# A two-layer decoder on one core: an order planned with tile shapes, top rows turned at full width, roots at both ends on ScalarE and VectorE

## The chip, the cores and the metric

The kernel runs on one core of a Trainium2 chip. Its engines are TensorE (matmuls into eight PSUM banks), VectorE, ScalarE, GpSimd and SyncE, which here issues nearly all DMAs. The metric is the device time of one execution in microseconds; lower is better.

## The reference

The input is x of 4 x 256 x 256 (batch, position, feature) and a context of 4 x 256 x 64. Six blocks follow one another, each added to its input and then normalised over the features (`layernorm(x + block(x))`):

1. latent attention with 32 heads: a projection to 192 query and 64 + 64 key values, a root-mean-square norm of both latents, rotated parts, causal softmax, output weights;
2. a mixture x = (1 - gamma) x + gamma A, where A is the symmetrised sigmoid of a similarity from the context, kept only where it is among the 76 largest of its row;
3. eight experts (one shared, seven routed, two chosen for each token), each up, silu gate, down;
4. causal attention with 16 heads of 16 values, with biases and rotation;
5. a bilinear block: softmax of a normalised similarity, scaled by rows gamma and beta;
6. a gated feed-forward with 1024 hidden values.

The last normalised x is the output. All is float32.

## The kernel before

All 1024 tokens stay in SBUF as 8 tiles of 128 rows (two for each batch). Weights come in by DMA, are split into a high and a low part (names ending in `_hi` and `_lo`), and most products are done as three matmuls hi*hi, hi*lo, lo*hi.

The work is written as steps such as `("s", b, g, half)`: scores of two heads of group g in batch b. `make_plan` (L396) declares for each step the engines it visits with an estimated time on each (`"PE 1.31, DVE 1.22, ACT:exp 1.8"`), the steps that it needs, and the buffers (banks, `probs`, `probsT`, ...) it holds. `Plan.arrange` (L301) is a list scheduler: it takes the engine whose next step can start soonest, and among the steps of this engine that can start within `NEAR[engine]` it takes the one with the highest level. The level is the longest chain of work behind the step, plus what the table `URGENT` (L176) adds for its name or its name and indices. The result is one order of steps for each engine, `ORDER`. `write_program` then emits for each engine its steps in this order; engines meet only by semaphores, so each engine works strictly in its order and stalls where a step isn't ready.

Steps that matter here, by the parts of the array their matmuls use:
- full width (128 rows, 128 columns): projections `q`, scores `s`, transposes `pT`, output `out`, experts `e_*`, `qkv`, `qkT`, feed-forward `f_*`;
- 128 rows, 64 columns: `w_v` (weights of values and output multiplied), `pv` (probabilities times the latent), `bi_kv`;
- 64 rows, 128 columns: `adj_sim`, `s1` and `st1` (scores of the second attention, once by rows for the maxima, once transposed for the exponentials), `ctx_tok`, `bi_sim`;
- 128 rows, 32 columns: `route_lin`, `pv1`;
- 64 rows, 64 columns: `adj_qk`, `ctx_T`.

In the planner before, TensorE knows nothing of these shapes. `NEAR["PE"]` is 0.

Top rows: `s1` writes the maxima of the rows of four heads into `top_tok` (128 x 2 x 4). `top_split` negates and splits them into `top_rows`, `top_T` transposes them (two transposes of 128 x 8, one for each row tile), ScalarE copies the result to `topT` (8 x 256), and four DMAs put it into rows of `qT1`, where `st1` uses it.

Roots: `down` computes the latents and their sums of squares (two halves h = 0, 1). `down_root` takes the reciprocal root on GpSimd: `power` with the exponent -0.5, then one Newton step (`newton_step`, L2384, four instructions). `down_scale` multiplies on GpSimd, ScalarE and VectorE; `down_T` transposes for TensorE. Each normalisation of x does `bn_stats`, `bn_aggr` and a small addition on VectorE (`statistics`, L1901), then `root` (L2355) on GpSimd. For the last batch the two tiles are done singly (`"first tile"`), and VectorE scales all output tiles (`out_norm`), each followed by a DMA to the output.

## Time and profile before

| | |
|---|---|
| time, median of 3 runs | 703.93 us (702.81 to 706.13) |
| span of the profiled execution | 700.4 us, 14717 instructions |
| the profiled execution's own time | not listed beside its span |
| TensorE busy | 680.6 us (97%), 4886 matmuls |
| VectorE, ScalarE, GpSimd busy | 531.1, 494.1, 394.8 us |
| DMA | 41.06 MB, mean 59 GB/s |

Read from a profile of one execution. Busy is the time in which an engine had an instruction in work; matmuls are pipelined and their ends are modelled, so the start times of matmuls are the better clock: the distance between two starts is what the first one cost. `PE` is TensorE, `PEld` its weight loads, `DVE` VectorE, `ACT` ScalarE, `POOL` GpSimd, `SP` SyncE. L1184, L1198, L2338, L2341 and the like are lines of helpers, so a line gathers operations of many steps; the tile names tell them apart.

### The profile page before, as it was taken

Reading aid. Unit: us, or ns where it says so; the run is one execution under the profiler, and the core shown is the slowest. Engines: PE = TensorE matmul, PEld = TensorE weight load, DVE = VectorE, ACT = ScalarE, POOL = GpSimd, SP = SyncE. Lnnn points to the kernel's source line nnn. Section 1 sums busy time; section 2 is a strip of 40 time slices with the busy share of each in tenths; the row PEclk is TensorE's granted clock in tenths of the full one; section 3 lists DMA queues with packets and bytes.
Section 4 is the critical chain, followed back from the end, with each engine's and each line's share of the span. In section 5 each row is a group of like instructions: output and inputs, shape, how many; then the busy total and the mean of one; then the engine's idle time right before and its main releaser. Section 6 shows DMA issues by size and latency. Waiting matters only on the chain.

```text
span 700.4 us, 14717 instructions
## 1 busy us (share of the span) xinstructions
PE 680.6 (97%) x4886; PEld 574.7 (82%) x4886; DVE 531.1 (76%) x1677; ACT 494.1 (71%) x1276; POOL 394.8 (56%) x657
## 2 busy tenths in 40 slices
PE   8899999999999999999998999999989999999995
PEld 6578998888888888888886888898977787678885
DVE  2678989888697869878889776565689777866537
ACT  3789774888659784788879786646766686857631
POOL 4659732885267741698867655544791322435625
PEclk9999999999999999999999999999999999999999
DMA  8671001240341401122012002111120000101201
GB/s 293 167 229 42 17 1 40 53 122 2 109 133 32 122 1 54 46 54 61 2 49 89 1 28 63 47 46 46 46 91 3 5 2 4 48 1 46 91 1 60
DMA packets 34418, 41.06 MB, mean 59 GB/s; under 512 B 6620, under 2 KB 27238, under 8 KB 34344
## 3 DMA queue, kind: packets, MB, share of 16 engines
q1 hardware_dynamic: 33800, 39.80, 19.4%
q8 instruction: 39, 0.64, 0.4%
q10 hardware_dynamic: 544, 0.33, 0.2%
q14 instruction: 35, 0.29, 0.1%
HBM read 30.02 MB, written 1.05 MB: 44 GB/s over the span
## 4 chain that ended last, share of the span: by engine, by line
PE 77%; POOL 9%; DVE 8%; issue 3%; DMA 1%; SPq 1%; ACT 0%; POOLq 0%; DVEq 0%
PE bank L1184 68%; PE bank L1198 8%; POOL stat L2341 3%; POOL qT L2341 1%; PE bank L1455 1%; POOL probs L2338 1%; DMA qT<-xT_plain 1%; DVE top_tok L2238 1%; POOL probs L2341 1%; POOL w_split_lo L2341 1%; DVE g_pair_lo L1896 1%; SPq L2622 1%; DVE y L1899 1%; POOL stat L2338 1%; DVE bn L1911 1%
## 5 line engine op out<-in xcount | busy, mean ns | idle before, releaser
L2338 POOL TENSOR_SCALAR probs<-probs,soft 128x256 f32<-128x256 f32 (+1 forms) x256 | 104.5, 429 | 48.4 <-DVE soft L2031 46.7
L1686 ACT ACTIVATE probs<-probs,soft 128x256 f32<-128x256 f32 (+1 forms) x256 | 113.0, 447 | 13.5 <-DVE soft L2023 12.9
L1184 PE MATMUL bank<-xT_hi,w_split_hi 128*128 128x512 f32 x256 | 103.7, 405 | 3.5 <-POOL w_split_lo L2341 3.2
L2341 POOL TENSOR_TENSOR w_split_lo<-w_raw,w_split_hi 128x512 fp32r<-128x512 f32 (+2 forms) x57 | 72.3, 1275 | 55.1 <-ACT w_split_hi L1592 54.9
L1184 PE MATMUL bank<-xT_lo,w_split_hi 128*128 128x512 f32 x256 | 101.0, 394 | 0.0
L1184 PE MATMUL bank<-keyT,qT 128*128 128x256 f32 (+1 forms) x512 | 93.4, 330 | 0.5 <-POOL qT L2341 0.3
L2023 DVE CUSTOM_DVE_ANT_0 probs<-bank,mask 128x256 f32<-128x256 f32 (+1 forms) x256 | 78.9, 353 | 19.8 <-PE bank L1184 19.1
L1184 PEld LDWEIGHTS bank<-keyT,qT 128*128 128x128 f32 x512 | 81.8, 190 | 12.3 <-issue 2.5
L2341 POOL TENSOR_TENSOR qT<-qT,xT_plain 64x512 f32<-64x512 f32 x44 | 57.0, 1295 | 57.6 <-DMA qT<-xT_plain 55.5
L1184 PE MATMUL bank<-xT_hi,w_split_lo 128*128 128x512 f32 x192 | 75.9, 395 | 0.0
L1592 ACT ACTIVATE qT<-bank 64x512 f32<-64x512 f32 (+1 forms) x80 | 47.4, 592 | 33.1 <-PE bank L1184 30.6
L1592 ACT ACTIVATE probsT<-bank 128x384 f32<-128x384 f32 x128 | 53.9, 490 | 18.6 <-PE bank L1198 18.4
L2341 POOL TENSOR_TENSOR probs<-probs 128x512 f32<-128x512 f32 x32 | 44.3, 1396 | 31.6 <-ACT probs L1769 31.0
L1184 PEld LDWEIGHTS bank<-xT_hi,w_split_hi 128*128 128x128 f32 x256 | 48.5, 190 | 15.5 <-POOL w_split_lo L2341 3.9
L1184 PEld LDWEIGHTS bank<-xT_lo,w_split_hi 128*128 128x128 f32 x256 | 48.6, 190 | 9.0
L2341 POOL TENSOR_TENSOR stat<-stat,power 128x2 f32<-128x2 f32 (+3 forms) x29 | 24.5, 843 | 49.2 <-DVE stat L1892 49.0
L1184 PE MATMUL bank<-probsT,key_tok 128*64 128x256 f32 (+1 forms) x512 | 50.2, 335 | 0.0
L1184 PE MATMUL bank<-w_split_hi,g_pair_hi 128*128 128x256 f32 x176 | 49.9, 284 | 0.3 <-DVE g_pair_lo L1896 0.3
L1198 PE MATMUL bank<-identity,probs 128*128 128x128 f32 x384 | 50.1, 273 | 0.1
L1184 PE MATMUL bank<-w_split_hi,g_pair_lo 128*128 128x256 f32 x176 | 49.4, 281 | 0.0
L1184 PE MATMUL bank<-w_split_lo,g_pair_hi 128*128 128x256 f32 x176 | 49.4, 280 | 0.0
L1686 ACT ACTIVATION_READ_ACCUMULATOR probs<-probs,soft 128x1 f32 x256 | 49.0, 191 | 0.0
(240 smaller groups left out, 1822.0 us busy)
## 6 DMA issues: line engine op xcount, KB each, us to landing
qT<-xT_plain SPq DMA_DIRECT2D x88, 64.0 KB, 2.0
w_raw<-in_w_nopeT SPq DMA_DIRECT2D x8, 512.0 KB, 3.6
w_raw_heads<-in_w_o SPq DMA_DIRECT2D x8, 512.0 KB, 5.1
qT<-rope_buf SPq DMA_DIRECT2D x40, 64.0 KB, 2.0
w_raw<-in_w_gateT SPq DMA_DIRECT2D x8, 256.0 KB, 2.8
w_raw<-in_w_upT SPq DMA_DIRECT2D x8, 256.0 KB, 3.3
w_raw<-in_w_downT SPq DMA_DIRECT2D x8, 256.0 KB, 3.8
w_raw<-in_L_ffn_Wup SPq DMA_DIRECT2D x7, 256.0 KB, 2.8
```

Of the source, the lines that this page charges most:

```text
L1184: return t.matmul(out, lhsT, rhs, start=start, stop=stop, skip_group_check=shared)
L1198: return t.transpose(out, in_, ident[0:rows, 0:rows])
L1455: ins = t.transpose(out[:, t_ * S + i * P:t_ * S + (i + 1) * P].bitcast(F32R), rows_of_head(rows)[:, i, first:first + P], ident1)
L1592: return s.activation(out, in_, ACT.Copy, **kw)
L1686: ins = s.activation(p[:, at], p[:, at], ACT.Exp, bias=st[:, 0, r:r + 1], scale=-1.0, accum_out=st[:, 1, r:r + 1])
L1896: return v.tensor_tensor(out, in0, in1, op)
L1899: return v.scalar_tensor_tensor(out=out, in0=in0, scalar=s, in1=in1, op0=op0, op1=op1)
L1911: own(v.bn_stats(bn[place][:, i, 0:6], tile))
L2023: v.tensor_tensor_reduce(out=p[:, at], in0=bank_of(("s", b, g, h))[:, at], in1=mask, scale=-SCALE0, scalar=3.0e38, op0=ALU.add, op1=ALU.mi ...
L2238: v.reduce_max(top_tok[top1_turns.place[b, g]][:, :, 2 * p + j], two(bank_of(("s1", b, h))), AX).then_inc(top1.sem, 1)
L2338: return g_.tensor_scalar(out, in0, s1, s2, op0, op1)
L2341: return g_.tensor_tensor(out, in0, in1, op)
```

## The change

- `Plan` gets `MODE = 0.13` (us for a TensorE step whose tile shape differs from the step before) and `KEEP = 835` (added to the level of a TensorE step that keeps the shape); `NEAR["PE"]` goes from 0 to 0.15. The small-tile steps are declared with their shape (`PE:cols64`, `PE:rows64`, `PE:cols32`, `PE:quarter`) and with other times. Every entry of `URGENT` is replaced.
- `probsT` has 8 buffers of 128 x 384 in place of 6 of 128 x 512; a group takes four at once, and `pT` of the second half comes after that of the first.
- Top rows: `top_rows` is 128 x 128, zeroed once; its first 16 columns hold high and low parts of both row tiles; one full transpose replaces two.
- `down_root` is split: VectorE forms a quarter of the mean square plus epsilon (`down_var`), ScalarE takes its square root, VectorE makes the reciprocal root from both in four instructions (`root_of_quarter`). The last batch's normalisation does the same, one tile at a time, and its scaling stays on VectorE. The other batches' roots stay on GpSimd, and their output tiles are scaled by ScalarE.
- `last_table`: a square root of one column on ScalarE behind the last `f_up`.
- Some semaphores that signalled one event each are merged.

```diff
-    HOP, TABLE = 0.2, 1.3
-
-    NEAR = {"PE": 0.0, "ACT": 0.3, "DVE": 0.3, "POOL": 0.5, "SP": 0.3, "DMA": 0.1, "WAY": 0.0}
+    HOP, TABLE, MODE = 0.2, 1.3, 0.13
+    KEEP = 835
+
+    NEAR = {"PE": 0.15, "ACT": 0.3, "DVE": 0.3, "POOL": 0.5, "SP": 0.3, "DMA": 0.1, "WAY": 0.0}
...
                     t = max(ready, free[engine], since)
-                    if kind and kind != table:
+                    if engine == "PE":
+                        t += self.MODE * (kind != tile)
+                    elif kind and kind != table:
                         t += self.TABLE
...
+            def stays(step):
+                engine, _, kind = self.parts[step][running[step][0]]
+                return engine == "PE" and kind == tile
+
             t, step, engine, taken = max((c for c in could if c[2] == soonest[2] and c[0] <= near),
-                                         key=lambda c: (level[c[1]], -c[0]))
+                                         key=lambda c: (level[c[1]] + self.KEEP * stays(c[1]), -c[0]))
...
-        stage(("down_root", h), "DVE 0.2, POOL 2.2", ("down", h), ("zero",))
+        stage(("down_var", h), "DVE 0.2, ACT 0.25", ("down", h))
+        stage(("down_root", h), "DVE 0.75", ("down_var", h))
...
-        stage(("w_v", g), "PE 1, ACT 0.6, DVE 0.6", ("load", g), *before,
+        stage(("w_v", g), "PE:cols64 0.8, ACT 0.6, DVE 0.6", ("load", g), *before,
...
-                      + [Hold("probsT", (b, g, h), By(("pv", b, g), "PE")) for h in heads], items=2)
-            stage(("pv", b, g), "PE 1.5, ACT 0.57, DVE 0.6", ("pT", b, g, 0), ("pT", b, g, 1),
+                      + [Hold("probsT", (b, g, h), By(("pv", b, g), "PE")) for h in range(GH) if half == 0], items=2)
+            stage(("pv", b, g), "PE:cols64 1.22, ACT 0.57, DVE 0.6", ("pT", b, g, 0), ("pT", b, g, 1),
...
-                stage(("s1", b, g, p), "PE 0.5, DVE 1.2", ("qkT", b, g), ("consts",),
+                stage(("s1", b, g, p), "PE:rows64 0.46, DVE 1.2", ("qkT", b, g), ("consts",),
...
-            stage(("pv1", b, g), "PE 1.02, ACT 0.45", *[("st1", b, g, p) for p in range(GH // 2)], ("v1", b), *every_expert,
+            stage(("pv1", b, g), "PE:cols32 0.88, ACT 0.45", *[("st1", b, g, p) for p in range(GH // 2)], ("v1", b), *every_expert,
...
+    stage(("last_table",), "ACT:sqrt 0.2", By(("f_up", NHALF - 1, HT - 1), "ACT"))
...
-                for i in range(TB):
-                    ins = transpose(out[0:2 * GH, i * P:(i + 1) * P],
-                                    plain(top_rows[top1_turns.place[b, g]][:, i, :, :]).rearrange("p c h -> p (c h)"))
-                ins.then_inc(topT_ready.sem, 1)
+                transpose(out[:, 0:P], plain(top_rows[top1_turns.place[b, g]][:, :])).then_inc(topT_ready.sem, 1)
...
+            elif name == "down_var":
+                h, = k
+                place = in_stat.place["down", h]
+                w.wait_ge(*low_seeded[h])
+                s.activation(stat[place][:, 2, :], stat[place][:, 0, :], ACT.Sqrt).then_inc(sqrt_taken.sem, 1)
...
+        def root_of_quarter(quarter, half, r):
+
+            own(v.reciprocal(r, half))
+            w.wait_ge(*own.now)
+            own(tt(r, r, quarter, ALU.mult))
+            w.wait_ge(*own.now)
+            own(tt(r, r, half, ALU.add))
+            w.wait_ge(*own.now)
+            return v.reciprocal(r, r)
...
                 for i, t in enumerate(batch_tiles(b)):
-                    w.wait_ge(*(newton["first tile"] if (b, i) == (B - 1, 0) else newton["out_stats", b]))
-                    ts(x[:, t, :], y[:, t, :], bn[place][:, i, 6:7], stat[place][:, 1, i:i + 1], ALU.subtract,
-                       ALU.mult).then_inc(out_normed.sem, 1)
+                    quarter, r, half = (stat[place][:, j, i:i + 1] for j in range(3))
+                    w.wait_ge(*sqrt_taken["last", i])
+                    own(root_of_quarter(quarter, half, r))
+                    w.wait_ge(*own.now)
+                    ts(x[:, t, :], y[:, t, :], bn[place][:, i, 6:7], r, ALU.subtract, ALU.mult).then_inc(last_normed.sem, 1)
```

## Rows read from the trace of the kernel before

**Rows 1.** Busy us and share of each engine; the last chain by engine.

```profile
PE 680.6 (97%) x4886; PEld 574.7 (82%) x4886; DVE 531.1 (76%) x1677; ACT 494.1 (71%) x1276; POOL 394.8 (56%) x657
...
PE 77%; POOL 9%; DVE 8%; issue 3%; DMA 1%; SPq 1%; ACT 0%; POOLq 0%; DVEq 0%
```

**Rows 2.** Windows: stretch, length, busy PE, PEld, DVE, ACT, POOL; clock, DMA, GB/s.

```profile
300.00:350.00 50.00, 50.00 (x390) 43.81 (x388) 41.98 (x171) 42.74 (x144) 43.25 (x82) 1.00 0.14 37
350.00:400.00 50.00, 46.99 (x323) 39.23 (x323) 42.34 (x118) 41.81 (x73) 33.69 (x67) 1.00 0.16 49
...
500.00:550.00 50.00, 46.86 (x445) 38.43 (x443) 43.95 (x93) 31.77 (x69) 29.42 (x34) 1.00 0.16 50
...
650.00:700.40 50.40, 42.49 (x259) 37.62 (x257) 27.01 (x58) 19.22 (x35) 22.50 (x42) 0.97 0.16 53
```

**Rows 3.** TensorE's waits: total us, times, longest.

```profile
PE bank L1184 <- POOL w_split_lo L2341: 3.2, 2, 1.8
...
PE bank L1184 <- ACT topT L1592: 0.5, 1, 0.5
```

**Rows 4.** TensorE in order of time: start, us, tile shape (rows*columns), operands, count.

```profile
17.31 1.08 PE L1184 MATMUL bank<-w_raw_heads 128*64 128x256 f32 x8
...
58.73 0.38 PE L1198 MATMUL bank<-identity,probs 128*128 128x128 f32 x2
59.04 0.66 PE L1184 MATMUL bank<-probsT,key_tok 128*64 128x256 f32 x4
...
61.74 0.38 PE L1184 MATMUL bank<-keyT,qT 128*128 128x128 f32 x2
61.96 0.82 PE L1198 MATMUL bank<-identity,probs 128*128 128x128 f32 x6
...
635.80 1.13 PE L1184 MATMUL bank<-kvT,outT 64*128 64x256 f32 x4
636.86 0.38 PE L1184 MATMUL bank<-w_split_hi,g_pair_hi 128*128 128x256 f32 x1
```

**Rows 5.** The same, in the second attention.

```profile
519.35 0.50 PE L1184 MATMUL bank<-kT,qT 64*128 64x256 f32 x4
...
539.25 0.38 PE L1198 MATMUL bank<-identity,top_rows 128*8 128x128 f32 x2
539.47 0.38 PE L1198 MATMUL bank<-identity,ctx 128*128 128x128 f32 x2
```

**Rows 6.** Single instructions by group: busy us, mean ns (first row: min/median/max ns).

```profile
L1592 ACT ACTIVATE top_rows<-top_tok x16: 191/210/212, 520.6 to 602.9; 128x8 fp32r<-128x8 f32 x16
...
L2253 DVE RECIPROCAL ctx_inv<-bank 128x8 f32<-128x8 f32 x16 | 3.2, 203 | 2.6 <-PE bank L1198 2.2
...
L1892 DVE TENSOR_SCALAR stat<-sums 128x8 f32<-128x8 f32 x2 | 0.3, 165 | 0.1
...
L1592 ACT ACT_TABLE_LOAD x1 | 1.3, 1283 | 1.8 <-issue 1.8
...
L2338 POOL TENSOR_SCALAR probs<-probs,soft 128x256 f32<-128x256 f32 (+1 forms) x256 | 104.5, 429 | 48.4 <-DVE soft L2031 46.7
```

**Rows 7.** The front in order of time; then GpSimd's small steps; then a window.

```profile
19.34 1.85 POOL L2341 TENSOR_TENSOR stat<-stat,power 128x8 f32<-128x8 f32 x1
...
21.20 1.39 DVE L1899 SCALAR_TENSOR_TENSOR xT_lo<-bank,q_ln,xT_hi 128x512 fp32r<-128x512 f32 x2
...
24.66 0.50 PE L1184 MATMUL bank<-xT_hi,w_split_hi 128*128 128x512 f32 x1 [1.82 <-POOL w_split_lo L2341]
...
L2341 POOL TENSOR_TENSOR stat<-stat 128x8 f32<-128x8 f32 x6 | 1.2, 202 | 0.5
...
25.10:28.40 3.30, 3.30 (x10) 2.52 (x9) 1.50 (x3) 0.91 (x2) 2.44 (x5) 0.50 0.29 34
```

**Rows 8.** The tail on VectorE in order of time.

```profile
695.28 0.15 DVE L1892 TENSOR_SCALAR stat<-bn 128x1 f32<-128x1 f32 x1
...
697.75 0.41 DVE L1893 TENSOR_SCALAR x<-y,bn,stat 128x256 f32<-128x256 f32 x1 [1.18 <-POOL stat L2341]
```

More of the change, by code:

```diff
@@ L301, in arrange @@
     def arrange(self):
-        level, ends, starts, table = self.levels(), {}, {}, ""
+        level, ends, starts, table, tile = self.levels(), {}, {}, "", ""
         free = defaultdict(float)
@@ L874, in write_program @@
     bi_exp = signal("bi_exp", keys("sim_max"))
+    out_normed = signal("out_normed", keys("out_norm", range(TB)))
     f_silu = signal("f_silu", keys("f_up"))
@@ L1856, in scalar_program @@
                 norm_rows(("sim_mix", b), batch_tiles(b))
+            elif name == "last_table":
+                w.wait_ge(*landed("identity"))
+                s.activation(last_root[:, 0:1], ident[:, 0:1], ACT.Sqrt)
+            elif name == "out_stats":
+                place = in_stat.place[step]
+                for i in range(TB):
+                    w.wait_ge(*seeded["first tile" if i == 0 else step])
+                    s.activation(stat[place][:, 2, i:i + 1], stat[place][:, 0, i:i + 1], ACT.Sqrt).then_inc(sqrt_taken.sem, 1)
+            elif name == "out_norm":
+                b, = k
+                place = in_stat.place["out_stats", b]
+                w.wait_ge(*newton["out_stats", b])
+                for i, t in enumerate(batch_tiles(b)):
+                    s.activation(x[:, t, :], y[:, t, :], ACT.Identity, bias=stat[place][:, 3, i:i + 1],
+                                 scale=stat[place][:, 1, i:i + 1]).then_inc(out_normed.sem, 1)
             elif name == "bi_kv":
@@ L2422, in pool_program @@
                 g_.memset(router_rows[:, :, :], 0.0).then_inc(zeroed.sem, 1)
-            elif name == "down_root":
-                h, = k
-                ve, r, s_ = (stat[in_stat.place["down", h]][:, j, :] for j in range(3))
-                w.wait_ge(*zeroed["zero"])
-                w.wait_ge(*low_seeded[h])
-                own(tt(r, ve, power[:, :], ALU.pow))
-                newton_step(r, s_, ve).then_inc(low_rsqrt.sem, 1)
             elif name == "down_rope":
@@ L2495, in pool_program @@
                     own(g_.memset(t[:, :, :], 1.0))
+                for t in top_rows:
+                    own(g_.memset(plain(t[:, :]), 0.0))
                 for t in (q_rows, k_rows):
```

276 lines of the change are left out of this document (141 added, 135 removed), and 43 rows, old and new, of the table URGENT.

## The prediction

> **What bounds the kernel now.** I read the engine totals first. TensorE is busy 680.6 of 700.4 us, VectorE 531.1, ScalarE 494.1, GpSimd 394.8 [rows 1]; by engine the chain that ended last is 77% TensorE [rows 1]. So it is a matmul-bound kernel, and an edit is worth what it takes out of TensorE's own stream, out of its waits, or out of the two ends. The windows say where the waits are [rows 2]: 300 to 350 us has none (50.00 of 50 us), 350 to 400 lacks 3.0, 500 to 550 lacks 3.1, and the last 50.4 us hold 7.9 us without a matmul, nearly all of it the tail. The list of waits puts a name to the largest: TensorE waits 3.2 us in two pieces for GpSimd's w_split_lo, 1.8 the longer, and only 0.5 us in all for the copy of the top rows [rows 3]. Full busy time isn't full speed, however, so I went to single matmuls.
>
> **A change of tile shape costs about 90 ns.** Two 128x128 transposes that begin at 61.74 (scores, same shape) are followed by the next group at 61.96: 0.22 us for two, 0.11 each. The two at 58.73 are followed by a 128*64 group at 59.04: 0.31 us, so 0.09 more. On leaving it is no less: the four 64*128 matmuls of 256 columns at 635.80 are followed at 636.86, 1.06 us for four of 0.22 us (twice a 128-column one), 0.18 more, of which I take half for the way out [rows 4]. Going through TensorE's records in order of start I count 183 changes of shape; the first is into the 128*64 group at 17.31 and the last at 636.86 us [rows 4]. Of them 89 lie before 400 us, most around the 128*64 stretches (38 stretches for 40 steps pv and w_v), and 94 between 510 and 637 us, where scores of the second attention (64*128, 33 stretches for 64 steps s1 and st1) alternate with pv1 (128*32, 13 stretches for 16 steps) and full-width work. 183 x 0.09 = 16.5 us of the span is spent on changes, nothing of which shows as idle.
> The Trainium skill (TensorEngine Tiling (Array Packing), Tiling Modes, Key Properties) says that changing the tiling mode drains TensorE; the trace agrees, with the 0.09 us above. By its list of modes a matmul of 8 columns would count as another mode than full width, and here the trace differs for transposes: see the top rows below.
>
> **The change, part by part.**
> *The order.* The planner gets a price of 0.13 us for a changed tile shape, a bonus of 835 on the level of a step that keeps the shape, a window of 0.15 us (before: 0) in which the more urgent TensorE step may be taken, lower prices for small-tile steps, and wholly new urgencies. The number of matmuls stays. What can be merged? Context products come one per (batch, group) and each needs its own two transposes; with room for two groups of transposed probabilities at once (8 places taken four at a time, before 6 taken two at a time) a few more pv and w_v may stand together: I take 4 stretches fewer of 38, 8 changes. In the second attention the 33 stretches often hold one step, four score products and their four masks, as at 519.35 [rows 5], while several steps are ready together whenever a (batch, group) has its rows; there I take 33 to 23 and 13 to 10, 26 changes. Sum 34 x 0.09 = 3.1 us, all on the path, as TensorE has no idle time there that would hide it. Bounds: 0 changes fewer (0 us) and, at the other end, half of all (92 x 0.09 = 8.3 us). Waits between steps are re-dealt by the new order; they can't fall by much more than the 6.1 us of the two stretches with most of them [rows 2], and I take 0, because nothing in the trace says whether the new order is better or worse in this.
> *Top rows at full width.* Now two transposes of 128x8 for each of 16 groups; after: one of 128x128. They cost 0.11 us each: two from 539.25 to 539.47, and the full-width transposes behind them begin without a gap, so they are no change of shape today [rows 5]. The gain is 16 x 0.11 = 1.8 us. The ScalarE copy of the negated maxima (210 ns [rows 6]) and VectorE's keep their size; the copy out has 128 columns for 256; four row DMAs of unchanged bytes stay, from four partitions each for two; three more GpSimd memsets lie in rows1, ahead of the second attention, in which GpSimd works 29.4 of 50 us [rows 2]. Bounds: 0 (if st1 waited for the DMA anyway) to 1.8; I take 1.8, since TensorE's waits of that kind are 0.5 us in all [rows 3].
> By the mode list of the Trainium skill (the same page) the narrow transposes would each be a change, and turning them at full width would save up to 32 x 0.09 = 2.9 us on top; the trace shows no such gap, so I don't count it.
> *Roots at the start.* Before, the second half's root on GpSimd is the power (1.85 us at 19.34) and four small steps of 0.2 us, some 2.8 us with the hand-overs; the scaling and then w_split_lo stand behind it, for which TensorE waits 1.82 us until 24.66 [rows 7]. After: one ScalarE square root of 128x8 (0.21 us by [rows 6]) and four VectorE steps at about 0.2 us each (reciprocal 0.20, small scalar step 0.17, plus the hand-over [rows 6]): 1.1 us for 2.8, so GpSimd comes to w_split_lo 1.7 us earlier. The next thing late would be xT_lo on VectorE, ready at 22.59, before TensorE falls idle at 22.84 [rows 7]. So 1.7 us of the wait go. Right behind that wait the granted clock is 0.50 from 25.1 to 28.4 us [rows 7], the lower of the two levels; 3.3 us at half speed costs 1.7 us. It fell after the engine had idled; with the idle time gone it may stay, and I count half, 0.8 us. What the first half's root wins is hidden: TensorE has w_v until 18.39 [rows 4] before it needs it. Bounds of the start: 0 to 3.5 us.
> Against it: square root needs a table. A table load takes 1.28 us [rows 6]; now one at the very front serves everything up to the routing. After there is at least one more, in front of the first square root or of the first exponential. Bounds for it: 0 (beside idle ScalarE) to 1.3 us; 0 taken, as ScalarE is busy only 71% of the span [rows 1].
> The Trainium skill (ScalarE: Activation LUTs, sections on table sets and on what a table load costs) says square root and exponential stand in different sets, and gives 1283 ns of load and 1380 ns of drain for a switch; by it the price would be 2.7 us of ScalarE. The load's 1283 ns stand in the trace; a drain beside them no run here shows.
> *Roots at the end.* Now VectorE's second seed ends at 695.43 and, behind GpSimd's root, the last scaling is 697.75 to 698.16 [rows 8]. After, VectorE does everything in order: from 695.43 four steps (0.8) and scaling (0.41) for the first tile, the same for the second, 697.85. Gain 0.3 us; the square roots finish beside it. The table for them is loaded behind the last SiLU, while TensorE does the last products. The six other output tiles are scaled by ScalarE in place of VectorE, off the path. Bounds: -0.5 (a step 0.1 slower eight times over) to +1.0.
> *The rest* (merged semaphores, probabilities' buffers of the same total size) costs nothing: no instruction is added by it.
>
> **Sum.** 3.1 + 1.8 + 1.7 + 0.8 + 0.3 = 7.7 us from the profiled span of 700.4 gives 692.7. The runs' median is 703.93, which is 3.5 us above that span; the profiled execution's own time isn't listed, so I carry the difference over: 696.2, stated as 696.
>
> **Rivals.**
> *A. The order doesn't group* (or what it groups it pays back in waits): 1.8 + 1.7 + 0.8 + 0.3 = 4.6 us, 699.3. For it: the bonus only helps where two steps of one shape are ready at once. Against: single-step stretches are common [rows 5].
> *B. The front turns against itself.* The first half's square root and its four VectorE steps stand in order in queues that also hold the second half's copies and squares; GpSimd had nothing beside them. Stuck behind these, with a table load of 1.3 us in front, the start loses 1.3 us in place of winning 2.5: 696.2 + 3.8 = 700.0. For it: both queues are in order. Against: w_q and w_v cover part of it.
> *C. Slower.* The new urgencies put the softmax work late. GpSimd is busy 43.3 of 50 us from 300 to 350, the stretch that ends in the statistics for which TensorE then waits (350 to 400 lacks 3.0) [rows 2]. A group (four heads) has 8 scalings of 0.43 us, 3.4 us [rows 6]; two groups more in this stretch fill it (6.8 us of room), each further one delays the routing by 3.4 us. This decides from the third group on; with six it is 20.6 - 6.7 = 13.9 us: 696.2 + 13.9 = 710. For it: all urgencies are replaced, and keeping a shape puts off score steps, which feed that chain. Against: TensorE is without waits in the same stretch, so the softmax work has kept ahead of it.
> *D. The waits of the middle shrink too*, by 4 of the 6.1 us of rows 2, for the corrected prices of small-tile steps let the planner see them: 692.
>
> **How the numbers follow.** Forecast 0.47 (its own range 693 to 699), D 0.12, A 0.16, B 0.10, C 0.15. I keep C that high because an order has hundreds of places and I can weigh one. 0.5% is 3.5 us, about what a measurement of this kernel can tell from no change, so the borders are 700.4 and 707.4. Faster: the forecast, D, and most of A and B, 0.70; same: the rest of A and B and the mild part of C, 0.17; slower: the rest of C, 0.13. The range of 8 in 10 runs from 689 (half of the changes gone) to 704 (C with three or four groups).
>
> **What would show it.** Right: fewer than 160 changes of shape, each still 0.09 us; 16 matmuls fewer; no wait of 1.8 us before 25 us and no stretch at clock 0.50 there; TensorE busy some 5 us less; the last scaling ends 2.4 us behind the last seed (now 2.7). Wrong: about 183 changes; TensorE idle clearly above its present 19.8 us, with GpSimd or VectorE named in 350 to 400 or 500 to 550; a table load between the first squares and the first scaling.

## The result, and the profile after

The changed kernel takes 705.68 us (704.07 to 708.87, 20 runs) where the one before took 702.49 us beside it on the same chip; the ratio is 1.0046, interval 1.0036 to 1.0056. It is slower by about 3.2 us, and the forecast was 696.0. Of what I had counted, the gain of the order is there and the rest is smaller than summed; what I had set to nothing, the waits and the clock behind them, is larger than the whole sum.

The profiled execution of the kernel after took 706.34 us, its span is 704.5 us. The page's engine totals and its row of granted clock in 40 slices:

```profile
PE 679.4 (96%) x4870; PEld 578.1 (82%) x4870; DVE 540.1 (77%) x1687; ACT 499.9 (71%) x1288; POOL 387.9 (55%) x646
...
PEclk9989999999999999999999999999998999999999
```

Against [rows 1] TensorE has 16 matmuls fewer and 1.2 us less busy time in a span 4.1 us longer. The two eights in the clock row (slices of 17.6 us; the third and the thirty-first) already say that part of the busy time is slow.

The windows of the kernel after, the same stretches as [rows 2], with the start added, which of before reads 24.89 busy at clock 0.93:

```profile
25.00:50.00 25.00, 22.32 (x90) 16.39 (x91) 14.75 (x45) 16.46 (x38) 9.97 (x11) 0.86 0.68 190
300.00:350.00 50.00, 50.00 (x388) 45.17 (x385) 42.21 (x172) 43.16 (x143) 40.12 (x85) 1.00 0.17 49
350.00:400.00 50.00, 46.30 (x299) 37.27 (x296) 41.20 (x105) 38.59 (x68) 35.99 (x65) 0.97 0.15 48
500.00:550.00 50.00, 45.88 (x419) 38.73 (x417) 41.95 (x85) 30.47 (x67) 25.75 (x29) 0.93 0.10 33
```

300 to 350 us is as full as before (GpSimd 40.1 against 43.3 us), so rival C's place holds nothing. Three other windows lost both busy time and clock. The list of TensorE's waits names them:

```profile
PE bank L1202 <- DVE xT_lo L1932: 3.3, 1, 3.3
PE bank L1216 <- DVE top_rows L1935: 2.7, 2, 2.2
PE bank L1202 <- POOL qT L2402: 2.7, 1, 2.7
...
PE bank L1202 <- DVE g_pair_lo L1932: 1.8, 2, 1.2
```

All four are new or longer (before had 0.3 us for qT, 0.4 for xT_lo, 0.3 for g_pair_lo and none for top_rows). A wait of 2.1 us for the bias row, left out here, is the start itself and the same in both kernels. Going through the matmul records in order of start, TensorE's idle time (a gap over 20 ns, the 2.1 us ahead of the first matmul included) is 17.9 us up to the last matmul; before it was 12.5. The clock record of the trace has half-clock stretches of 6.8 us at 40.2, 3.4 us at 374.7 and 6.8 us at 528.3, where before had one of 3.4 us at 25.1. The first two begin inside the first two of the long waits, the third 0.5 us behind the third; the wait of 1.2 us for g_pair_lo at 422 us has none. The 20 timed executions agree with the profiled one in this: their mean granted clock is 0.982 to 0.989.

**The first of them: SyncE's queue.** The front of the kernel after in order of time:

```profile
28.75 0.45 SPq L2583 DMA_DIRECT2D w_raw<-in_w_nopeT  x1
...
32.01 0.43 SPq L2589 DMA_DIRECT2D w_raw_heads<-in_w_o  x1
32.49 5.02 SPq L2662 DMA_DIRECT2D qT<-xT_plain  x8
...
38.52 3.92 POOL L2402 TENSOR_TENSOR qT<-qT,xT_plain 64x512 f32<-64x512 f32 x3 [12.44 <-DMA qT<-xT_plain]
...
41.16 1.22 PE L1202 MATMUL bank<-keyT,qT 128*128 128x256 f32 x2 [2.68 <-POOL qT L2402]
```

The new order has the load of the third group (seven issues, 28.75 to 32.44) ahead of the first swap of query rows. The swap was issued at 28.35 before and is now at 32.49; GpSimd adds its result from 38.52 where it did from 33.15, and the first scores start at 41.16 for 38.32.

**The second and third: VectorE's queue.** The engines in order of time around 374 us, then around 527 us:

```profile
371.46 1.37 DVE L1932 TENSOR_TENSOR router_buf<-iota,rt_stat 128x32 f32<-128x32 f32 x2
371.84 0.61 ACT L1607 ACTIVATE xT_hi<-bank 128x512 fp32r<-128x512 f32 x1
...
372.86 1.19 DVE L1935 SCALAR_TENSOR_TENSOR router_buf<-router_buf 128x32 f32<-128x32 f32 x1
373.97 0.68 DVE L1932 TENSOR_TENSOR xT_lo<-bank,xT_hi 128x512 fp32r<-128x512 f32 x1
...
374.80 0.77 PE L1202 MATMUL bank<-xT_hi,w_split_hi 128*128 128x512 f32 x1 [3.28 <-DVE xT_lo L1932]
375.36 0.63 PE L1202 MATMUL bank<-xT_lo,w_split_hi 128*128 128x512 f32 x1
375.79 0.63 PE L1202 MATMUL bank<-xT_hi,w_split_lo 128*128 128x512 f32 x1
```

```profile
525.05 1.28 DVE L2297 TENSOR_REDUCE top_tok<-bank 128x2 f32<-128x512 f32 x2
526.25 1.34 DVE L1932 TENSOR_TENSOR rope_tmp<-bank,rope 128x512 f32<-128x512 f32 x3
526.37 0.21 ACT L1607 ACTIVATE top_rows<-top_tok 128x8 fp32r<-128x8 f32 x1
527.51 0.16 DVE L1935 SCALAR_TENSOR_TENSOR top_rows<-top_tok,top_rows 128x8 fp32r<-128x8 f32 x1
...
527.77 0.30 PE L1216 MATMUL bank<-identity,top_rows 128*128 128x128 f32 x1 [2.23 <-DVE top_rows L1935]
```

At 374 the xT_lo that TensorE needs stands behind the routing's steps: its input xT_hi is written at 372.45, and it starts at 373.97, so VectorE's queue makes 1.5 of the 3.3 us. At 527 a step of 0.16 us stands behind three rotations: the last maxima are there at 526.3 and ScalarE's copy of them at 526.58, so the rotations make 0.9 of the 2.2 us. The rest of both waits is the chain from TensorE's own last products over ScalarE or VectorE back to TensorE; the order now leaves TensorE nothing to do beside it. Neither wait is new work. Behind the first the matmuls of 512 columns begin every 0.43 us; at full clock they begin every 0.23.

**Where the ends went.** On ScalarE and VectorE in the kernel after, the start and then the tail:

```profile
14.63 1.28 ACT L1644 ACT_TABLE_LOAD   x1
...
15.93 0.21 ACT L1644 ACTIVATE stat<-stat 128x8 f32<-128x8 f32 x1
```

```profile
698.79 0.15 DVE L1929 TENSOR_SCALAR stat<-bn 128x1 f32<-128x1 f32 x1
698.80 1.09 ACT L1891 ACTIVATE x<-y,stat 128x256 f32<-128x256 f32 x2 [4.57 <-POOL stat L2402]
...
699.80 0.28 ACT L1885 ACTIVATE stat<-stat 128x1 f32<-128x1 f32 x2
...
701.91 0.41 DVE L1929 TENSOR_SCALAR x<-y,bn,stat 128x256 f32<-128x256 f32 x1
```

The table load does stand between the squares and the first scaling. In the tail the square roots wait behind two scalings of ScalarE (698.80, 1.09 us), and the last scaling ends 3.4 us behind the end of the last seed, where I had written 2.4 and [rows 8] has 2.7. The tail from the end of the last matmul to the end is all the same 7.3 us for 7.2, because that seed comes 0.6 us sooner behind the last matmul.

**Shape changes.** TensorE in the second attention of the kernel after:

```profile
541.35 0.33 PE L1202 MATMUL bank<-mask,halves 64*128 64x128 f32 x4
541.52 0.45 PE L1202 MATMUL bank<-kT,qT 64*128 64x256 f32 x4
...
542.27 0.34 PE L1202 MATMUL bank<-mask,halves 64*128 64x128 f32 x4
542.53 1.09 PE L1202 MATMUL bank<-probs,v_tok 128*32 128x256 f32 x16
```

Four masks followed by the same shape take 0.17 us, followed by another shape 0.26: the 0.09 us of [rows 4] again. There are 143 changes for 183: 59 before 400 us (before 89), 84 behind 510 us (before 94).

### The profile page after: what moved, and what is told of

The parts are those of the page before. It is cut to its first block, busy times and chain, and to the rows that moved or that the text cites. A ratio compares the mean times of both kernels' runs of the same rounds, so it can differ in the third digit from the quotient of the medians.

```text
span 704.5 us, 14691 instructions
## 1 busy us (share of the span) xinstructions
PE 679.4 (96%) x4870; PEld 578.1 (82%) x4870; DVE 540.1 (77%) x1687; ACT 499.9 (71%) x1288; POOL 387.9 (55%) x646
## 4 chain that ended last, share of the span: by engine, by line
PE 78%; DVE 5%; POOL 5%; SPq 5%; issue 3%; ACT 2%; DMA 1%; POOLq 0%; ACTq 0%; DVEq 0%
PE bank L1202 70%; PE bank L1216 8%; SPq L2576 2%; POOL stat L2402 1%; PE bank L1473 1%; DMA qT<-xT_plain 1%; POOL probs L2402 1%; POOL w_split_lo L2402 1%; POOL qT L2402 1%; POOL probs L2399 1%; DVE probs L2082 1%; ACT x L1614 1%; SPq L2587 1%; DVE bn L1955 1%; DVE sim L2141 1%
## 5 line engine op out<-in xcount | busy, mean ns | idle before, releaser
L1202 PE MATMUL bank<-xT_hi,w_split_hi 128*128 128x512 f32 x256 | 105.3, 411 | 4.1 <-DVE xT_lo L1932 3.3
L1202 PE MATMUL bank<-keyT,qT 128*128 128x256 f32 (+1 forms) x512 | 95.2, 333 | 3.0 <-POOL qT L2402 2.7
L2402 POOL TENSOR_TENSOR w_split_lo<-w_raw,w_split_hi 128x512 fp32r<-128x512 f32 (+2 forms) x57 | 73.9, 1307 | 37.6 <-ACT w_split_hi L1607 37.3
L2402 POOL TENSOR_TENSOR probs<-probs 128x512 f32<-128x512 f32 x32 | 42.3, 1334 | 39.9 <-ACT probs L1789 38.8
L2402 POOL TENSOR_TENSOR stat<-stat,power 128x2 f32<-128x2 f32 (+1 forms) x25 | 20.5, 819 | 50.6 <-DVE stat L1928 50.0
L1216 PEld LDWEIGHTS bank<-identity,probs 128*128 128x128 f32 x384 | 43.2, 141 | 4.8 <-POOL probs L2399 2.4
```

The source lines that it names most:

```text
L1202: return t.matmul(out, lhsT, rhs, start=start, stop=stop, skip_group_check=shared)
L1216: return t.transpose(out, in_, ident[0:rows, 0:rows])
L2402: return g_.tensor_tensor(out, in0, in1, op)
```

## The experiments

Each kernel was timed against the kernel before on the same chip, the median in us and the ratio with its interval. "Idle" is TensorE's idle time up to the last matmul, as above. "Stretch" is one of granted clock 0.50, which is 1.2 of 2.4 GHz; the one in the tail, which every kernel has, is left out. Both are of the one profiled execution. Of the timed ones only the mean granted clock is on record, and it tells how much half clock there was but not where: each profiled execution with 0.997 or 0.998 had none, each with 0.996 or less had at least one. The useless matmuls are products into a bank that the step's own first product overwrites.

### The order alone taken back, and its two causes

order_before: the kernel after, with the planner of before (its costs, urgencies and six places for transposed probabilities); the new steps of the roots are put into the order by hand.

```diff
-    HOP, TABLE, MODE = 0.2, 1.3, 0.13
-    KEEP = 835
-
-    NEAR = {"PE": 0.15, "ACT": 0.3, "DVE": 0.3, "POOL": 0.5, "SP": 0.3, "DMA": 0.1, "WAY": 0.0}
+    HOP, TABLE = 0.2, 1.3
+
+    NEAR = {"PE": 0.0, "ACT": 0.3, "DVE": 0.3, "POOL": 0.5, "SP": 0.3, "DMA": 0.1, "WAY": 0.0}
...
+put("ACT", ("down_var", 0), ("down", 0))
+put("DVE", ("down_root", 0), ("down_var", 0))
```

> The changed kernel with the old order written back: TensorE's sequence of steps, the loads and the buffers' turns are those of before; kept are the top rows at full width, the roots at the start on ScalarE and VectorE, the tail on ScalarE and VectorE. Theory 1 (the new order is at fault, the other edits gain): 16 top-row transposes fewer, 1.8 us, the wait at 23 us shorter, the tail 0.1 to 0.3 us: 2 to 4 us below the kernel before, some 699.5 us. Theory 2 (the other edits cost, by the table load of 1.28 us and VectorE and ScalarE stalled for each other at the front): at or above the kernel before, 703 to 706 us, and then the new order is worth something.

load_behind: SyncE's load of the third group behind the second key swap.

```diff
+ORDER["SP"].remove(("load", 2))
+ORDER["SP"].insert(ORDER["SP"].index(("key_swap", 1)) + 1, ("load", 2))
```

> The changed kernel with one move on SyncE: the seven weight DMAs of group 2 behind the three first query swaps and the second key swap, in place of ahead of them. Theory 1 (the first scores wait 2.7 us because the swap of the first query was issued at 32.5 us behind these DMAs, and the clock falls to 0.50 for 6.8 us behind that wait): the swap goes out at about 28.8, the wait at 41.2 us goes (2.7 us) and with it the stretch at half clock (2.5 to 3 us): 5 to 6 us below the changed kernel, about 700 us. Theory 2 (the swap isn't what ends last; ScalarE's copies or GpSimd's adds are): 0 to 1 us.

fill_waits: the three large waits filled with useless full-size matmuls.

```diff
+FILL = {("s", 0, 0, 0): 11, LATE_U: 13, TOPS[2]: 9}
...
+        def fill(out, rhs):
+            for _ in range(FILL.get(step, 0)):
+                mm(out, ones1[:, :], rhs)
```

> The changed kernel with matmuls of no use in front of three steps that TensorE waits for: 11 of 512 columns ahead of the first scores (2.5 us in a wait of 2.7), 13 ahead of the first expert product of the second half (3.0 in 3.3), 9 ahead of the third top-row transpose (2.1 in 2.2). The waits stay, TensorE is busy in them. Theory 1 (the granted clock falls to 0.50 because TensorE has been idle): the stretches of 6.8, 3.4 and 6.8 us at half clock go, 7 to 8.5 us gained less up to 1 us of overhang: about 698 us. Theory 2 (the fall comes from somewhere else in the stream): no gain, 705 to 707 us.

before_fill: the same on the kernel before, in its 1.8 us wait at 22.8 us.

```diff
+                if step == FIRST_Q:
+                    for _ in range(7):
+                        mm(wait_bank(("q", n, g, p, "rot"))[:, :], ones1[:, :], bias1[:, 0:2 * D])
```

> The kernel before with 7 such matmuls (1.6 us) ahead of the first query product, in the wait of 1.82 us at 22.8 us. Theory 1: the half-clock stretch from 25.1 to 28.4 us goes, 1.7 us gained: about 701 us, ratio 0.9975. Theory 2: no gain.

| kernel | median | ratio | idle | stretches (start, length) |
|---|---|---|---|---|
| order_before | 704.20 | 1.0015 [1.0000, 1.0030] | 13.0 | 43.3 3.4; 514.4 3.4 |
| load_behind | 705.18 | 1.0036 [1.0013, 1.0059] | 15.0 | 38.5 6.8; 185.3 3.4; 376.4 3.4; 526.6 6.8 |
| fill_waits | 701.76 | 0.9968 [0.9950, 0.9986] | 9.4 | 37.6 6.8 |
| before_fill | 703.14 | 1.0002 [0.9984, 1.0020] | 12.8 | 46.7 3.4 |

In the same code the order of after costs 0.3% against the order of before. load_behind gained 0.5 us, within its interval, where I had expected 5 to 6. fill_waits adds 33 matmuls of no use and is 0.8% faster than the kernel after, 4 us by the medians where I had expected nearly 8: the stretches at 374 and 528 us come with the waits, and go when TensorE has work in them. The windows of fill_waits over those two places:

```profile
374.50:378.00 3.50, 3.27 (x27) 2.52 (x30) 2.71 (x7) 1.94 (x4) 0.76 (x1) 1.00 0.02 5
528.00:534.50 6.50, 6.50 (x66) 5.07 (x65) 5.34 (x11) 6.36 (x13) 2.71 (x3) 1.00 0.01 2
```

The early stretch did not obey. load_behind has no wait of 2.68 us at 41 us any more, and still the clock falls:

```profile
38.00:40.00 2.00, 2.00 (x9) 1.36 (x8) 1.13 (x5) 1.27 (x4) 0.63 (x1) 0.63 1.04 282
40.00:42.00 2.00, 2.00 (x6) 1.60 (x6) 0.11 (x1) 1.09 (x3) 0.00 (x0) 0.50 0.83 296
```

TensorE is busy in the whole of both windows, and in the 2 us ahead of them. What it had run, in order of time in load_behind:

```profile
32.99 3.64 PE L1204 MATMUL bank<-ctxT,w_qk_x 64*64 64x512 f32 x8
36.56 2.00 PE L1204 MATMUL bank<-w_kv_x,ctxT 64*128 64x64 f32 x16
38.40 1.88 PE L1204 MATMUL bank<-qk_x 64*128 64x256 f32 x4
40.21 2.93 PE L1204 MATMUL bank<-keyT,qT 128*128 128x256 f32 x8
```

The new order had put four small groups in a row (adj_qk twice, ctx_tok, adj_sim); in the kernel before, VectorE takes up ctx_tok's result at 361 us, in the kernel after at 38. load_behind's second stretch, at 185.3 us, stands behind four waits of 0.25 to 0.32 us for probabilities.

before_fill gained nothing (1.7 us was expected): its stretch at 25 us goes and one comes at 46.7 us, at a wait of 2.6 us for qT that before did not have. This isn't the filling's doing alone. small_run and mix_run below have the program of before up to 110 us, without any filling, and in them too the wait of 1.82 us at 22 us left the clock at 1.00 and a wait for qT with a stretch stands near 46. The two waits in mix_run:

```profile
23.39 0.50 PE L1184 MATMUL bank<-xT_hi,w_split_hi 128*128 128x512 f32 x1 [1.82 <-POOL w_split_lo L2348]
...
46.22 2.93 PE L1184 MATMUL bank<-keyT,qT 128*128 128x256 f32 x8 [2.65 <-POOL qT L2348]
```

So the same instructions with the same wait lose the clock in one execution and keep it in another, and when they keep it, the time won is lost again at qT.

### The row of small products

apart: the row parted by a query product and by the first scores, load_behind's change kept. apart_fill: with the fills at 375 and 528 us too.

```diff
+for _e, _moved in (("PE", [(("q", 1, 0, 0), ("adj_qk", 1)), (("adj_sim", 0), ("s", 0, 0, 0))]),
+                   ("ACT", [(("q_lat", 1, 0, 0), ("adj_qk", 1)), (("adj_sim", 0), ("s", 0, 0, 0))])):
+    for _s, _after in _moved:
+        ORDER[_e].remove(_s)
+        ORDER[_e].insert(ORDER[_e].index(_after) + 1, _s)
```

> The kernel after, with SyncE's load of the third group behind the second key swap (as in load_behind) and, on TensorE and ScalarE, the fourth q product put between the small adjacency products and the first scores put ahead of adj_sim: no four small groups stand in a row any more. In load_behind TensorE's clock fell to 0.50 at 38.5 us though it had hardly waited; ahead of it stood 7 us of products of 64 rows or 64 columns. Theory 'small products in a row take the clock': the stretch of 6.8 us at half clock near 38 us is gone or halved, the time falls by 1.7 to 3.4 us against load_behind (705.2), to 702 to 703.5. Rival 'it is the idle time earlier (0.8 us at 25 us) or the place in time': the stretch stays at 35 to 45 us with its length and the time is as load_behind's, 704.5 to 706. The stretches near 376 and 527 us stay in both.

> The same, with 13 and 9 useless full matmuls in the waits before an e_u product near 375 us and before a transpose of top rows near 528 us, as in fill_waits, and none at the first scores. If the three stretches at half clock (6.8, 3.4 and 6.8 us) are what the order lost, this is the fastest kernel so far: about 701.8 (fill_waits) less up to 3, so 698.5 to 701. If the early stretch is not of the small products' making, it is as fill_waits, 701 to 702.5. The gains of the two waits were shown once; a third outcome, a new stretch elsewhere of 3.4 us, costs 1.7.

small_run, full_run, mix_run, tok_run: the kernel before with useless products at one place near 113 us where it has neither waits nor a low clock: 8 of adj_qk's shape; 32 full ones; adj_qk's, ctx_tok's and adj_sim's in a row; 32 of ctx_tok's shape.

```diff
+                    if step == ("q", 1, 2, 0) and kind == 1:
+                        for i in range(32):                       # tok_run
+                            mm(out[:, i % 8 * CTX:(i % 8 + 1) * CTX], ctxT[:, i % 8 * P:(i % 8 + 1) * P], w_kv_x[:, :])
```

> The kernel before with 8 useless products of 64 rows and 64 columns (the operands and shape of adj_qk; about 7.3 us at the 0.46 us per recorded half that adj_qk took) in front of a q product near 113 us, where TensorE has no waits and the clock of before stood at 1.00. Theory 'a run of small products takes the clock by itself': a stretch at 0.50 begins during or right behind them, with no idle time of TensorE ahead of it. Rival 'the clock falls only behind idle time': no stretch at 0.50 between 100 and 140 us. The work added costs about 7.3 us either way, a stretch of 3.4 or 6.8 us another 1.7 to 3.4.

> The control of small_run: at the same place 32 useless products of the full 128 rows and 128 columns with 512 columns streamed, about 7.3 us at 0.23 us each. Both theories expect no stretch at 0.50 between 100 and 140 us; if one comes, it is the place or the delay of the other engines' work and not the small shape. About 7.3 us longer than before.

> The kernel before with the row that stood ahead of the early stretch, made of useless products at one place near 113 us: 4 of adj_qk's shape (64 rows, 64 columns), 8 of ctx_tok's (64 rows, 64 columns streamed) and 2 of adj_sim's, some 6.6 us, no wait ahead of them. Theory 'the row takes the clock': a stretch at 0.50 begins in it or right behind it (113 to 121 us). Rival 'it takes the start's own state too (the first copies, the wait of 0.8 us, the transfers)': no stretch between 100 and 140 us. About 6 us longer than before, 3.4 at half clock would add 1.7.

> The same place, 32 useless products of ctx_tok's shape alone (each 64 rows by 128 columns of weights with 64 columns streamed, recorded as two of 0.12 us or so): about 8 us. If products that stream few columns are what takes the clock, a stretch at 0.50 begins in them and they take longer than 0.125 us each; if not, none between 100 and 140 us, as in small_run.

| kernel | median | ratio | stretches |
|---|---|---|---|
| apart | 704.95 | 1.0038 [1.0022, 1.0053] | 184.5 3.4; 375.6 3.4; 525.8 6.8 |
| apart_fill | 700.80 | 0.9974 [0.9959, 0.9990] | none |
| small_run | 709.85 | 1.0104 [1.0085, 1.0123] | 47.2 3.4 |
| full_run | 707.98 | 1.0077 [1.0060, 1.0095] | 24.1 3.4 |
| mix_run | 709.26 | 1.0091 [1.0074, 1.0109] | 46.0 3.4; 121.1 3.4 |
| tok_run | 713.48 | 1.0151 [1.0134, 1.0169] | 23.6 3.4; 115.7 13.7 |

Parted, the row leaves no early stretch in either profiled execution, though apart has a wait of 0.63 us at 39 us. The time was not the 1.7 to 3.4 us better that I expected: the ratios are 1.0038 and 1.0036. Its idle time is 1.9 us more than load_behind's, which takes back more than half of what the clock gave. Nor does the row always make a stretch: four of fill_waits' twelve executions have a mean clock of 0.997 or 0.998 with the row in place, against 13 of the 24 of the parted and filled kernel (apart_fill and its repeat below). The theory's first form, that small tiles do it, fell with small_run: 7.08 us of 64*64 tiles, each with 512 columns, and the clock stays at 1.00. The next two runs, mix_run and tok_run, have the stretch. small_run's window over its useless products, then mix_run's over the row and what follows:

```profile
115.00:122.00 7.00, 7.00 (x22) 2.60 (x21) 2.66 (x8) 0.00 (x0) 2.52 (x2) 1.00 0.05 13
```

```profile
118.00:121.00 3.00, 3.00 (x21) 2.61 (x22) 0.00 (x0) 0.00 (x0) 0.00 (x0) 1.00 0.02 5
121.00:124.50 3.50, 3.50 (x10) 2.67 (x10) 1.50 (x3) 0.00 (x0) 0.00 (x0) 0.52 0.00 0
```

And tok_run, in order of time and by windows:

```profile
112.61 11.11 PE L1184 MATMUL bank<-w_kv_x,ctxT 64*128 64x64 f32 x64
```

```profile
112.00:115.00 3.00, 3.00 (x27) 2.87 (x27) 2.60 (x8) 0.00 (x0) 1.77 (x2) 1.00 0.11 28
115.00:116.00 1.00, 1.00 (x10) 1.00 (x10) 0.00 (x0) 0.00 (x0) 0.76 (x1) 0.86 0.00 0
116.00:124.00 8.00, 8.00 (x38) 7.88 (x38) 0.00 (x0) 0.00 (x0) 0.00 (x0) 0.50 0.00 0
124.00:129.00 5.00, 5.00 (x15) 4.03 (x15) 2.73 (x8) 0.68 (x2) 0.00 (x0) 0.50 0.11 25
```

TensorE never waits here, and its clock falls from 1.00 to 0.50 while it runs products of 64 rows that stream 64 columns each; it stays there for 13.7 us. The 64 recorded products take 11.1 us, 0.17 each, where the same took 0.125 in mix_run at full clock. The second execution of tok_run (mean clock 0.988, the profiled one 0.986) lost about as much. Whether the 64 rows or the 64 columns matter isn't separated here, as no run streamed 64 columns through 128 rows for as long. So the order's grouping, which put ctx_tok behind adj_qk for the sake of the tile shape, can make the early stretch without any wait, and in load_behind it did.

### The other edits, one by one

order_before_fill: order_before with its waits at 43.9, 374.7 and 513.6 us filled. top_only: the kernel before with the top rows in one transpose. roots_only: order_before with the top rows as before.

```diff
+FILL = {("s", 0, 0, 1): 6, ("e_u", 2, 0): 6, ("qkT", 0, 0): 6}      # order_before_fill
...
```

```diff
-                for i in range(TB):                                 # top_only, and the layout around it
-                    ins = transpose(out[0:2 * GH, i * P:(i + 1) * P], ...)
+                transpose(out[:, 0:P], plain(top_rows[top1_turns.place[b, g]][:, :])).then_inc(topT_ready.sem, 1)
```

> The kernel after with the order of before (order_before, 704.2) and 6 useless full matmuls in each of its waits at 43.9, 374.7 and 513.6 us. There two stretches of 3.4 us at half clock stood at 43.3 and 514.4 us. Theory 'the other edits save about 3 us and the clock takes it back': both stretches go, 704.2 - 3.4 = 700.8, between 699.8 and 701.8, below before's 702.4. Rival 'the other edits save nothing': what the clock gives back is lost to the same waits a little later, 703 to 704.5.

> The kernel before with one part of the change alone: the top rows of the second attention turned in one full-width transpose instead of two narrow ones. 16 matmuls fewer and 32 narrow-shape changes the fewer or the same count less 16; my sum put 1.8 us on it. Theory 'it saves what was summed': 702.4 - 1.8 = 700.6 (0.9974). Rival 'the second attention waits on other engines, and what TensorE saves turns into waiting, with or without a clock stretch': 702 to 704, TensorE's busy time less by 1 to 2 us and its idle time more by as much.

> The kernel after with the order of before and the top rows as they were: of the change there is left only the roots at both ends by ScalarE and VectorE (and the signals they need). My sum put 1.7 us of waiting and 0.8 us of clock at the start and 0.3 us at the end on it. order_before, which has the top rows too, gained nothing (1.0015); top_only gained nothing either (1.0006). Theory 'the start's gain is taken back behind it': the wait of 1.8 us near 25 us and the half clock there are gone, and a wait for qT and a stretch of 3.4 us near 43 us stand in their place; 702 to 704, 1.000 to 1.003. Rival 'the start's gain stays, and it is the two parts together that lose it': 699 to 700.5 and no stretch near 43 us.

| kernel | median | ratio | idle | stretches |
|---|---|---|---|---|
| order_before_fill | 701.73 | 0.9984 [0.9970, 0.9999] | 9.3 | none |
| top_only | 702.76 | 1.0006 [0.9992, 1.0021] | 12.6 | 25.2 3.4 |
| roots_only | 703.91 | 1.0021 [1.0011, 1.0031] | 12.1 | 45.6 3.4; 516.6 6.8 |

The roots alone make the kernel slower. In roots_only the wait of 1.82 us ahead of the first query product has shrunk to 0.36, as forecast, and the next row is where it went:

```profile
23.07 0.47 PE L1212 MATMUL bank<-xT_hi,w_split_hi 128*128 128x512 f32 x1 [0.36 <-DVE xT_lo L1948]
44.86 2.27 PE L1212 MATMUL bank<-keyT,qT 128*128 128x256 f32 x8 [1.71 <-POOL qT L2415]
```

```profile
45.60:49.00 3.40, 3.40 (x14) 3.08 (x13) 2.48 (x14) 2.35 (x10) 3.26 (x5) 0.50 0.88 295
```

TensorE is ready for these scores at 43.15 us, 3.3 us sooner than before (46.4), but GpSimd starts on their qT only 1.6 us sooner (42.23 for 43.78), and TensorE waits for it. The stretch at 516.6 begins 2.2 us behind the start of the product that waited for q_rows (1.5 us), a wait that the kernel before has too without losing its clock there. The profiled execution is the slowest of the twelve; the median of their mean clock is 0.993, for 0.995 to 0.996 in most of before.

top_only: TensorE's record ends 0.8 us earlier than in before (692.4 for 693.2), and no gain could be measured; the interval leaves 0.6 us at the most. By the groups of the two kernels from 500 to 650 us, before and then top_only:

```profile
L1198 PE MATMUL bank<-identity,top_rows 128*8 128x128 f32 x32 | 6.0, 273 | 0.0
```

```profile
L1206 PE MATMUL bank<-identity,top_rows 128*128 128x128 f32 x16 | 4.8, 309 | 0.0
```

### What is left once the clock is kept

before_fill2: the kernel before with the waits at 22.8 and 46 us filled; before_fill3: that at 512 us too. apart_fill_again ran beside it. best (it is not the fastest; the name is older than the run): apart_fill with VectorE's bias step behind its w_v step.

```diff
+                    if step == ("qkT", 0, 0) and part == "q":           # before_fill3
+                        for _ in range(6):
+                            mm(out[:, :], ones1[:, :], bias1[:, 0:2 * D])
```

```diff
+ORDER["DVE"].remove(("consts",))                                      # best
+ORDER["DVE"].insert(ORDER["DVE"].index(("w_v", 1)) + 1, ("consts",))
```

> The kernel before with 7 useless full products in its wait at 22.8 us and 11 in the wait for qT near 46 us, where before_fill lost again what it had gained. Theory 'the filling alone gives the clock back': no stretch at 0.50 but the last, 702.2 - 1.7 = 700.5 (0.9976), about what apart_fill and fill_waits gave (0.9974, 0.9968), and the change itself would be worth almost nothing. Rival 'the change's fewer shape changes and matmuls are worth 2 us or more once the clock is kept': before_fill2 stays at 701.5 to 702.5 and the filled versions of after are ahead of it by 0.2 to 0.3%.

> before_fill2 with 6 useless full products more in the wait of 1.46 us at 512 us, behind which its one stretch at 0.50 stood. With no stretch but the last one: 1.7 us less than before_fill2, 0.9975 of before, if half-clock time is all that counts; then the change with its clock kept (0.9968 to 0.9974) is worth nothing. Rival: it stays at 0.9985 to 1.000, and the change with its clock kept is worth 0.1 to 0.3%.

> The same kernel as apart_fill, beside before_fill3 on one chip. Expected 0.9974 again within 0.0015. If it is below before_fill3 by 0.1% or more, the change's edits are worth that much once TensorE's clock is kept; if the two agree within 0.1%, they are not.

> apart_fill (700.8, 0.9974) with one move more: VectorE's bias step (consts, 2.24 us at 36.9 us) behind its w_v step of the second group. In apart_fill TensorE's first scores waited 1.31 us at 39.6 us for the bank that this w_v step empties. If that was the wait, the first scores start 1.3 us earlier and the time is 699.5 (0.9955); rival: GpSimd's qT (5.3 us of adding from 32.8 us) is as late, and the gain is under 0.5 us.

| kernel | median | ratio | idle | stretches |
|---|---|---|---|---|
| before_fill2 | 701.94 | 0.9998 [0.9987, 1.0009] | 10.2 | 513.9 3.4 |
| before_fill3 | 701.28 | 0.9981 [0.9967, 0.9995] | 9.1 | none |
| apart_fill_again | 700.93 | 0.9977 [0.9961, 0.9993] | 12.5 | none |
| best | 701.57 | 0.9989 [0.9979, 0.9999] | 12.6 | none |

In before_fill2's profiled execution the stretch stands behind the wait at 512 us; six of its twelve executions have a mean clock of 0.998, and with all three waits filled eleven of twelve have 0.997 or 0.998. On one chip before_fill3 and apart_fill_again differ by 0.05% (701.28 and 700.93), far inside their intervals. But "none" in the table is true of the profiled execution alone: seven of apart_fill_again's twelve have a mean clock of 0.993 to 0.996, so the clock was not kept on both sides. Executions with a mean clock of 0.997 or more, which by the profiled ones had no stretch, compare like this:

| executions without a stretch | count | median | lowest to highest |
|---|---|---|---|
| before_fill3 | 11 of 12 | 701.27 | 700.48 to 701.81 |
| apart_fill_again, same chip | 5 of 12 | 699.75 | 697.91 to 700.77 |
| order_before_fill | 10 of 12 | 701.84 | 701.13 to 702.62 |
| apart_fill, same chip | 8 of 12 | 700.03 | 698.24 to 701.77 |

So with the clock kept the whole change (with the two moves of apart) is some 1.5 us faster than the kernel before, and the new order 1.8 us faster than the old one, though it idles more: apart_fill_again's profiled span is 698.0 us with 12.5 us idle, before_fill3's 700.0 with 9.1. The second pair has the top rows and the roots on both sides and differs in the order and the fillings. These are groups picked from the timed executions after the fact, few of them, and no run of their own. The fastest ratio stays fill_waits' 0.9968, which beats both kernels, and its interval overlaps that of before_fill3. best removed the wait of 1.31 us at 39.9 us and found one of 2.5 us for GpSimd's probabilities at 47.8; nine of its twelve executions have a mean clock of 0.992 to 0.996.

## Why the prediction was wrong

- **The failed step** is "Waits between steps are re-dealt by the new order; ... I take 0, because nothing in the trace says whether the new order is better or worse in this." The idle time rose by 5.4 us (12.5 to 17.9), and three new waits of 2.2 to 3.3 us stand for it. I had bounded only the gain of this step, by the 6.1 us that the two stretches had, and not its loss; a bound below was owed. Rival C had a loss for it, in another place (GpSimd from 300 to 350 us, still without waits).
- **What the waits cost twice.** The half clock behind a wait was in the prediction for the old wait at 25 us (0.8 us as a gain) and missing for any new one. The stretches hold 12.4 us more of matmul time (5.8 + 3.3 + 6.7 less 3.4), and since the 512-column matmuls begin every 0.43 instead of 0.23 us there, 0.20/0.43 of it, an estimate of 5.7 us, is lost. fill_waits shows that the two later ones hang on their waits. Of the first, load_behind, mix_run and tok_run show that it can come behind small products alone; in the kernel after it has both ahead of it.
- **The order, 3.1 us:** right in mechanism: 40 changes fewer, 3.6 us at 0.09 each. That the sum is near is partly luck, for it came where I looked least: 30 of the 40 lie before 400 us (I had 8 there) and 10 behind 510 us (I had 26).
- **Top rows, 1.8 us:** 16 matmuls are gone, but in top_only the trace shows 0.8 us and the timing at most 0.6. A full-width transpose was costed like a narrow one; the groups have 309 ns for 273.
- **The start, 2.5 us:** the wait ahead of the first query product shrank to 0.36 us in roots_only, and the stretch at 25 us is gone. It was given back 20 us later, at the wait for qT (1.71 us) with 3.4 us at half clock. In after the wait is 0.83 us and for ScalarE's keyT; with the new order ahead of it, the first query product starts at 24.94 us, 0.3 later than before. "What is late next" was asked of the first query product and not of the first scores. Rival B's place was right (a table load of 1.28 us in front of the root), its price small: in roots_only the load lies at 11.4 us, early enough.
- **The end, 0.3 us:** the last scaling ends 3.4 us behind the last seed and not 2.4, as the roots stand behind ScalarE's scalings; the tail as a whole is no shorter (7.3 us for 7.2).
- **The level.** I carried over 3.5 us between the profiled span and the runs' median. An execution's time is 1.8 to 2.0 us above its span in every run on record, so the sum should have led to 694.5; the 3.5 came from a median of three runs (703.93) that 20 runs put at 702.49.
- **The account** up to the end of the last matmul, after less before: idle +5.4, half clock +5.7, shape changes -3.6, top rows -0.8, in all +6.7; the traces differ by +4.1 (693.2 to 697.3). 2.6 us of this are not accounted for. Waits that fall inside a stretch are taken out of it; what else is counted double I could not find.

Not settled: why one and the same wait costs the clock in one execution and not in another, as that of 1.82 us at 22 us does and does not in the program of before, and that of 1.5 us at 512 us in roots_only, order_before and before_fill2 against before, top_only and before_fill. Where a stretch lies is known of single profiled executions only.

## What to carry to other kernels

A new order is to be costed by the waits that it makes as well as by what it groups, with a bound for the loss: read each in-order queue (SyncE's transfers and VectorE's small steps above all) for a short step on which the matmuls wait and which a long one could come to precede. A wait of TensorE of 2 to 3 us cost about as much again in half clock here (5.7 us of half clock beside 5.4 of idle), and a saving upstream of the next late operand only moves the wait; before crediting it, follow it to the next two consumers. To find what an edit is worth beside its effect on the clock, fill the waits of both kernels with useless matmuls, look at the mean granted clock of every timed execution and not only at one profile, and compare executions in which it was kept.

## What the runs showed of the hardware

- TensorE's clock fell to half with TensorE busy all the time, on products of 64 rows streaming 64 columns each (tok_run, 1.00 to 0.50 at 115.7 us, for 13.7 us); it did not fall on 7.1 us of 64*64 tiles streaming 512 columns (small_run), nor on 7.7 us of full tiles (full_run).
- Stretches in or behind waits of 1.4 to 3.5 us were 3.4 or 6.8 us long. The same wait of 1.82 us, in the same instructions, had one in before, full_run and tok_run and none in small_run and mix_run.
- The total of half clock differs between executions of one kernel: apart_fill_again's mean clock is 0.993 to 0.998, and its executions at 0.997 or more have a median of 699.75 us, the others of 702.15.
- Useless matmuls in a wait can pay: 33 of them took 0.8% off the kernel after (1.0046 to 0.9968).
- A switch of ScalarE's table for the square root showed 1.28 us and nothing beside it: the load begins at 14.63 and the square root at 15.93 us.
